# A recurrent layer and the network after it: from two stages to one

## The reference, cut to what matters

```python
q = x @ q_w.T; k = x @ k_w.T; v = x @ v_w.T          # 16 heads of 8
lc = sigmoid(tanh(x @ cs_w1.T + cs_b1) @ cs_w2.T + cs_b2)
lam = clip(sigmoid(decay_params) * (1 + 0.2 * lc), 0, 0.9995)
state = state * lam_t + k_t[:, None] * v_t[None, :]   # per head, 8 x 8, over 1024 tokens
y_t = q_t @ state;  s = y @ o_w.T
top1 = argmax(softmax(x @ gate_W.T + gate_b))         # one of 8 experts
inter = relu(x @ wi_W.T + wi_b + (x @ lora_A[top1].T) @ lora_B[top1].T)
g = silu(inter @ wo_W.T + wo_b)                       # 512 hidden
out = x_in + s * g
```

## Time and profile before

| | us |
|---|---|
| median of 3 runs (lowest, highest) | 1789.2 (1782.86, 1791.3) |
| the profiled execution's own time | 1788.66 |
| its span, first to last instruction | 1786.8 |
| layer 0 (`before_heads`, `attend`) | about 1520 |
| `recur`, from its first to its last instruction | about 191 |
| `finish` | about 76 |

### The profile page before, as it was taken

One profiled execution on the slowest core, in us unless ns is written; L12 is line 12 of the kernel. 1 busy time (PEld: TensorE's weight loads), 2 busy tenths in 40 slices (PEclk: granted clock), 3 DMA queues, 4 the chain that ended last, 5 costly groups with the idle time before them and its releaser, 6 DMA issues. The chain is left out here.

```text
span 1786.8 us, 38903 instructions
## 1 busy us (share of the span) xinstructions
PE 1631.6 (91%) x11942; PEld 909.4 (51%) x12100; DVE 1498.1 (84%) x3033; ACT 1149.5 (64%) x1755; POOL 1400.4 (78%) x804
## 2 busy tenths in 40 slices
PE   4879989858999999999999999999999998899888
PEld 3435654423555555555555555555555554466566
DVE  8778978986898988989889898898988988778831
ACT  6536534537887777887788777788778877312133
POOL 5576846847999999999999999999999997545421
PEclk9899999988999999999999999999999999889999
DMA  5466856769899889889889889889889888100001
GB/s 164 127 183 191 226 154 169 197 203 189 173 199 212 186 189 219 186 177 234 187 175 232 177 188 225 182 186 220 191 184 222 189 177 174 46 0 1 1 7 42
DMA packets 732914, 294.09 MB, mean 165 GB/s; under 512 B 629088, under 2 KB 696674, under 8 KB 732848
## 3 DMA queue, kind: packets, MB, share of 16 engines
q1 hardware_dynamic: 730048, 289.80, 72.1%
q0 software_dynamic: 2048, 3.15, 0.9%
q10 hardware_dynamic: 768, 0.53, 0.1%
HBM read 101.34 MB, written 58.85 MB: 90 GB/s over the span
## 5 line engine op out<-in xcount | busy, mean ns | idle before, releaser
L1270 POOL TENSOR_TENSOR probs_lo<-probs 128x1024 bf16<-128x1024 f32 x512 | 953.6, 1895 | 80.5 <-ACT probs L1234 80.0
L1234 ACT ACTIVATE probs<-scores,neg_max 128x1024 f32<-128x1024 f32 x512 | 588.3, 1149 | 220.1 <-DVE neg_max L1152 211.4
L1152 DVE CUSTOM_DVE_ANT_0 scores<-score_ps,bias_tab 128x1024 f32<-128x1024 f32 x512 | 620.5, 1220 | 76.9 <-issue 69.8
L1082 PEld LDWEIGHTS turn_ps<-ident_bf,probs 128*128 128x128 bf16 x4096 | 261.2, 98 | 146.1 <-issue 55.9
L1066 PE MATMUL score_ps<-x 128*128 128x512 bf16 x866 | 273.9, 384 | 48.9 <-PEq L293 18.2
L1082 PE MATMUL turn_ps<-ident_bf,probs 128*128 128x128 bf16 x4096 | 314.4, 220 | 0.2
L1101 PE MATMUL pv_ps<-probs_t_hi,v_hi_lo 128*128 128x512 bf16 x1024 | 263.8, 381 | 0.3 <-DVE share L1184 0.3
L1241 ACT COPY probs_t_hi<-turn_ps 128x1024 bf16<-128x1024 bf16 x256 | 253.8, 991 | 0.0
L438 POOL TENSOR_TENSOR qk_parts<-rotated,qk_parts 128x1024 bf16<-128x1024 f32 x64 | 137.4, 2151 | 87.7 <-ACT qk_parts L871 87.3
L1167 DVE COPY probs_t_hi<-turn_ps 128x1024 bf16<-128x1024 bf16 x256 | 172.7, 675 | 0.8 <-PE turn_ps L1082 0.8
L1074 PE MATMUL score_ps<-x 64*128 64x512 bf16 x1024 | 155.9, 383 | 0.0
(11 more groups left out here) (218 smaller groups left out, 2316.3 us busy)
## 6 DMA issues: line engine op xcount, KB each, us to landing
x<-qk_parts SPq DMA_DIRECT2D x192, 256.0 KB, 3.3
qk_parts<-qk_parts SPq DMA_DIRECT2D x252, 128.0 KB, 2.6
v_hi_lo<-v_parts SPq DMA_DIRECT2D x64, 256.0 KB, 3.1
bias_tab<-bias_by_distance SPq DMA_DIRECT2D x64, 240.0 KB, 3.8
v_parts<-bias_tab SPq DMA_DIRECT2D x52, 256.0 KB, 3.0
probs_t_lo<-probs_lo SPq DMA_TRANSPOSE x512, 3.2
g<-in_x SPq DMA_DIRECT2D x4, 512.0 KB, 6.3
dispatch<-dispatched SPq DMA_DIRECT2D x8, 256.0 KB, 3.4
```

The costliest lines, as they stand in the source:

```text
L1082: mm = pe.transpose(tp[n % 2][:, k, :], PRB[n % NP][:, k * P:k * P + P], ident16[:])
L1152: v.tensor_tensor_reduce(SB[n % 2][:], sp_[n % 2][:], TB[s][:, j:j + S], -SCALE, 3.0e38, ALU.add, ALU.min, neg_max[:, n % 16:n % 16 + 1]). ...
L1234: act.activation(PR[n % NP][:], SB[n % 2][:], ACT.Exp, bias=neg_max[:, m:m + 1], scale=-1.0, accum_out=row_sum[:, m:m + 1]).then_inc(exped, 1)
L1270: g.tensor_tensor(LQ[n % NL][:], PR[n % NP][:], PRB[n % NP], ALU.subtract).then_inc(low_made, 1)
```

## The change

`recur` and `finish` become one block, `layer1`. The jobs between the steps are handed out by a new function, `steps_of_layer1`, which also spreads the network's jobs, `zt` (transposes of masked z), `hid` (a hidden tile) and `out` (an output block), over steps 4 to 31 by a weight of 1, 2 and 7. They use the two `aux_ps` banks too, since the made rows and the share hold the other six. A bank is free when its taker has it: ACT for most jobs, DVE for `v`, `zt` and `out`.

- From batch 1 on the repeated value rows are not made by an fp32 matmul. A job `v` makes the 128 values once; ACT and DVE and POOL split them into three bf16 parts (high on ACT, remainder on DVE, middle on ACT, low on POOL), 24 DMAs a batch (`stack`) put the three parts of one column under one another in 48 rows of `v_stacked`, and two bf16 matmuls with a pattern of ones (`head_rows`, made on POOL) repeat and add them.
- `best_gate` and `route` work on one batch each: `best_gate` behind steps 1, 4, 12, 20, `route` two steps later. ACT's exp is between them.
- The norm is applied by ACT (scale and shift a tile), no longer by DVE; POOL makes the shift.
- silu, the product and the sum are done by batch; of batches 0 to 2 the product and sum are POOL's (`add_share`), of the last one DVE's.
- Table loads on ACT from the start of layer 1 on: 3 before, 11 now.

The diff, cut to its core:

```diff
+def steps_of_layer1():
+
+    at = [[] for _ in range(FE * B)]
+    at[0] += [("q", 0, 0), ("q", 0, 1)]
+    at[1] += [("z", 0, 0)]
+    for b in range(1, B):
+        n = FE * (b - 1)
+        for f, jobs in enumerate(([("turn", b, 0), ("turn", b, 1)], [("z", b, 0), ("c1", b, 0)], [("c1", b, 1), ("k", b, 0)],
+                                  [("k", b, 1), ("c2", b, 0)], [("c2", b, 1)], [("q", b, 0)], [("q", b, 1)])):
+            at[n + f] += jobs
+    for b in range(1, B):
+        for c in range(2):
+            at[FE * (b - 1) + 1 + c].append(("v", b, c))
+    feed = [("zt", 0, 0)] + [("hid", 0, i) for i in range(FT)]
+    for j in range(NR):
+        if j + 1 < NR:
+            feed.append(("zt", j + 1, 0))
+        feed.append(("out", j, 0))
+        if j + 1 < NR:
+            feed += [("hid", j + 1, i) for i in range(FT)]
+    cost = {"zt": 1, "hid": 2, "out": 7}
+    total, done, span = sum(cost[job[0]] for job in feed), 0, FE * B - FFN_FROM
+    for job in feed:
+        at[FFN_FROM + done * span // total].append(job)
+        done += cost[job[0]]
...
         @block.sync
...
+            def stack(b):
+                sp.wait_ge(v_lo, 2 * b)
+                if b >= 3:
+                    sp.wait_ge(made, FE * (b - 1))
+                for f in range(FE):
+                    for p in range(3):
+                        to = 64 * (f % 2) + H * p
+                        sp.dma_start(VP[b % 2][to:to + H, f // 2, :],
+                                     V3[H * f:H * f + H, p, :]).then_inc(vp_in[b % 2], DMA)
...
         @block.vector
...
+            for n in range(N):
+                scan(n)
+                for job in steps[n]:
+                    take(job)
+                if n % FE == 2 and n // FE + 2 < B:
+                    stats(n // FE + 2)
+                if n in GATE_AT:
+                    best_gate(GATE_AT.index(n))
+                if n - 2 in GATE_AT:
+                    route(GATE_AT.index(n - 2))
+                if n == 1:
+                    split_lora()
...
         @block.gpsimd
...
+                g.tensor_tensor(WT[:, n % 2, :], SC[:, n % 2, :], QT[:, b % 2, :], ALU.mult).then_inc(weighed, 1)
+                if n == 0:
+                    head_rows()
+                for kind, i, c in steps[n - 1] if n >= 1 else ():
+                    if kind == "v":
+                        v_low(i, c)
+                if f == 3 and b + 2 < B:
+                    rstd(b + 2)
+                if n == 4:
+                    join(3)
+                if n - 1 in SILU_AT[:B - 1]:
+                    add_share(SILU_AT.index(n - 1))
...
         @block.scalar
...
+            norm(0)
+            for job in first:
+                take(job)
...
+            norm(1)
+            act.wait_ge(fin_in, 7 * DMA)
+            for n in range(N):
+                for job in steps[n]:
+                    if job[0] != "out":
+                        take(job)
+                for kind, b, c in steps[n]:
+                    if kind == "v":
+                        middle(b, c)
+                if n % FE == 1 and n >= FE:
+                    take_share(n // FE - 1)
+                if n - 1 in GATE_AT:
...
+                    act.activation(lg, lg, ACT.Exp).then_inc(exp_ready, 1)
+                if n % FE == 5 and n // FE + 2 < B:
+                    norm(n // FE + 2)
+                if n in SILU_AT:
+                    gate(SILU_AT.index(n))
...
         @block.tensor
...
+                    if n < FE:
+                        mm = pe.matmul(pj[n % 2][:, half(c)], wv[:, f, :], tokens(b, c),
+                                       start=True, stop=True)
+                    else:
+                        mm = pe.matmul(pj[n % 2][:, half(c)], SEL[at, :, :].rearrange("r h e -> r (h e)"),
+                                       VP[b % 2][at, f // 2, half(c)], start=True, stop=True)
...
+                elif kind == "zt":
+                    pe.wait_ge(zm_ready, b // 2 + 1)
+                    for t in range(4):
+                        mm = pe.transpose(dst[0:3 * ER, t * P:t * P + P], ZM[:, 4 * (b % 4) + t, :], K.ident[:])
+                elif kind == "hid":
+                    pe.wait_ge(by_dve, dve_nth["zt", b, 0])
```

More of the change, by code:

```diff
@@ L42 @@
 DMA = 16
+FE, FFN_FROM = 8, 4
 MAGIC = 12582912.0
@@ L1322, in recur, with bank, half, rows @@
     ax = [ps(f"aux_ps{i}", [P, CH]) for i in range(2)]
-    FE = 8
     N = B * FE
[L1325 to L1341, removed]
+    first, steps = steps_of_layer1()
+    jobs = first + [job for step in steps for job in step]
+    place = {job: a for a, job in enumerate(jobs)}
+    step_of = {job: n for n, step in enumerate(steps) for job in step}
+    act_takes = [job for job in jobs if job[0] != "out"]
+    dve_takes = [job for job in jobs if job[0] in ("v", "zt", "out")]
+    act_nth = {job: k + 1 for k, job in enumerate(act_takes)}
+    dve_nth = {job: k + 1 for k, job in enumerate(dve_takes)}
+    GATE_AT = [1] + [FE * (b - 1) + 4 for b in range(1, B)]
+    SILU_AT = [step_of["out", 2 * b + 1, 0] + 1 for b in range(B)]
+    def bank(job):
+        return ax[place[job] % 2]
+    def half(c):
+        return slice(c * CH, c * CH + CH)
+    def rows(b):
+        return slice(b * BT, b * BT + BT)
+    def tokens(b, c):
+        return XNT[:, b * S + c * CH:b * S + c * CH + CH]
+    def vp_due(b):
+        return 3 * DMA * FE * len(range(2 - b % 2, b + 1, 2))
     with nc.Block() as block:
@@ L1386, in route @@
-            def route():
-                v.wait_ge(exp_ready, 1)
+                for t in range(b * BT, b * BT + BT):
+                    ins = v.bn_stats(st.six[:, t, :], X1[:, t, :])
+                ch.link(ins)
+                for t in range(b * BT, b * BT + BT):
+                    ins = v.bn_aggr(st.mean_var[:, t, :], st.six[:, t, :])
+                ch.link(ins)
+                ch.link(v.tensor_scalar(back[:, rows(b)], st.mean_var[:, rows(b), 0], -1.0, None, ALU.mult))
+                v.tensor_scalar(st.var[:, rows(b)], st.mean_var[:, rows(b), 1], 1e-5, None, ALU.add).then_inc(var_ready, 1)
@@ new lines, in take, with middle, gate @@
+                ins.then_inc(by_act, 1)
+            def middle(b, c):
+                act.wait_ge(by_dve, dve_nth["v", b, c])
+                act.copy(V3[:, 1, half(c)], VR[:, half(c)]).then_inc(v_mid, 1)
+            def take_share(b):
+                act.wait_ge(shared, FE * (b + 1))
+                act.wait_ge(joined, B + 1)
+                act.copy(S1[:, rows(b), :], so[:]).then_inc(s1_out, 1)
+            def gate(b):
+                act.wait_ge(by_dve, dve_nth["out", 2 * b + 1, 0])
+                act.activation(Y[:, rows(b), :], Y[:, rows(b), :], ACT.Silu).then_inc(gated, 1)
@@ L1532, in _ @@
+            if SILU_AT[B - 1] >= N:
+                gate(B - 1)
         @block.tensor
```

423 lines of the change are left out of this document (194 added, 229 removed).

## The result

The changed kernel takes 1766.2 us (median of 4 runs, 1762.2 to 1770.7), the kernel before 1789.7 in the same comparison: ratio **0.9885**, 95% interval 0.9862 to 0.9908, so faster by 1.2%. Forecast were 1761 us and a range of 1738 to 1783. The profiled execution took 1762.21 us, its span is 1760.5.

A forecast was written before the change was run, and what follows sets the result against it. PE was taken to set the pace of both stages. Ideal span 1733.9 us, plus 10.9 for the first z turn, 5 for clock and 9.3 for ACT's order, gave 1759.1; with 1.9 over span, 1761 us, range 1738 to 1783.

The forecast's parts named there:

- PE's work: From step 1 on, PE's priced jobs sum to 181.2 us, with bf16 made rows at 0.43 instead of 1.72.
- waits and half clock there: Added to PE's work: first z turn and hidden tile 10.9 us, low clock 5, ACT's order 9.3.
- rest: The end, behind step 31's made rows: hand-overs +2.8 us, then last products, sums and store 5.5.
- a turn: PE's transposes, read as 8 passes where a share has 16, priced at 0.45 us.
- The first z turn: In step 4, PE waits 7.0 us for route, then 3.8 at the hidden tile: together +10.9, +5 to +15.
- the stalled addition: Route's second operation on DVE, beside POOL's 2.35 us product, takes 2.49 us instead of some 0.4.
- Clock: PE's clock falls after the two close waits in step 4, counted as one: +5 us, between 0 and 12.
- ACT in order: ACT's added work and table loads free PE's banks late, in steps 10, 11 and 17 to 19: +9.3 us, 3 to 18.
- v by DMA: Stacking by 24 transfers a batch, 0.45 us each to issue, 11 us, costs nothing; later batches have some 20 us to spare.
- Rival 2: DVE becomes a partner in the bound; 11 takes of bank results at 1.5 us each give 1777. Chance 0.18.
- Rivals 3 and 4: PE idles at every bank DVE takes, 1798, chance 0.04; stacking transfers land one after another, 1817, chance 0.03.
- PE's 26 us of work: PE's passes over 24 steps: 31 us leave with the cheaper made rows, 5 come with the v jobs.

The follow-up runs named there:

- full rows: Changed kernel with the made rows of batches 1 to 3 contracted over all 128 rows, unused ones zero, instead of 48: 1755.7 us, ratio 0.9836.
- Parts alone: Changed kernel's bf16 parts, ACT norm and routing by batch, but the network in its own stage behind the recurrence as before: 1789.5 us, ratio 1.0018 to the kernel before.
- first jobs later: Changed kernel with 128-row made rows and padded lam network, plus the network's first jobs moved one or two steps later: 1764.5 us, ratio 0.9878.
- the padded network: Kernel with 128-row made rows, first z turn in step 5 and other network jobs from step 6, plus lam network zero-padded to 128 columns and rows: 1759.7 us.

## Why the prediction came out right

The forecast of 1761 lies 5 us under the median and 1.2 under the profiled run; the mechanism held, and two terms were off in opposite directions, so that the sum came out this near is in part luck. Forecast for the layer: 1759.1 - 1520.75 = 238.35. Measured: 245.17. The profiled span of 1760.5 agrees better than that only because the unchanged code ahead was 5.4 us shorter in this profile.

| stretch | forecast | measured | off |
|---|---|---|---|
| start to made rows of step 1 | 23.65 | 22.81 | -0.8 |
| PE's work, to made rows of step 31 | 175.4 | 187.7 | +12.3 |
| waits and half clock there | 25.2 | 18.5 | -6.7 |
| rest | 14.1 | 16.2 | +2.1 |

(The measured work is 206.19 less 15.5 of waits less some 3 of half clock at step 4; the forecast one is 181.2 less the last three shares and a pair of made rows.)

**PE's work, the mis-sized term.** The step was: "They contract 48 rows, the row's 96; I take its price." 0.43 became 0.53, and the pieces on both sides pay as well: 24 x 0.3 = 7 us, of which full rows gave back 6. The 12 us by kind of job, start to start and without the half clock of step 4: shares +2.7, made rows +2.4, k, q and v jobs +1.7, 12 c1 and c2 jobs +1.3 (1.02 where I had 0.92), z and turns +1.1, hidden tiles +2.6, outputs +0.3. The 7 are the first two and the jobs that stand behind made rows. The hidden tiles pay beside waits too: one that starts behind a wait took 0.96 instead of 0.86, and a low-rank part with a wait behind it 0.38 instead of 0.22. The reading of a turn was off as well: it has 4 passes (x4 in the timeline) and not 8; 0.45 was right for a z turn (0.44), but a pair of turns of normed tiles took 1.09. I had read the earlier trace rows, where a 96-row tile stands between tiles of 128, as the nearest row; the nearest was in the earlier trace rows, where two c1 jobs (32 columns) and the share behind them cost more than a q pair and its share. The Trainium skill (TensorEngine Tiling (Array Packing), "Key Properties") says that changing the tiling mode, and not just the tile, drains TensorE. The trace fits that, with a price of 0.1 us on each of the pieces around a change, but doesn't show a drain as such. Nothing of the kind shows at 96 rows: a hidden tile's low-rank part is 0.22 in both the earlier trace rows and the new stage.

**The first z turn** was forecast to wait 7.0 and the hidden tile 3.8; they waited 4.4 and 3.1. The routing ended 49.2 us into the layer instead of 52.0: it took 5.1 us from scan 3's end, forecast were 7.3. The 2.38 us of the stalled addition (L1466, forecast 2.49) were right, and the comparison behind it (L1468) was held up by POOL's v part, 0.82 instead of 0.22; pow, 1.65 us beside DVE, stopped nothing: the four small products (L1470) took 0.26 to 0.27 each beside it, as they do alone. The Trainium skill (SBUF — State Buffer, "SBUF: two separate sides") has the port pair of VectorE and GpSimd as a lock held for a whole instruction. The addition ends with POOL's product, 2.38 against 2.34, which agrees; the four products beside pow don't, and there the measurement decides.

**Clock**: +5 forecast; some 3 at step 4, and 1.6 at the last share, which was not forecast and stands in the row "rest".

**ACT in order**: 9.3 forecast; waits for lam, cs_hidden, k_t, xn_t and fhid 6.0, batch 3's turn 1.2, banks of v 0.8, so 8.0. Removing the switches gave 3.4 to 4.9. By place: steps 17 to 19, where the forecast had 4, gave 2.3, and steps 10 and 11, where it had 2.8, gave 1.8.

**v by DMA**: nothing, as forecast, but with luck. An issue took 0.63 us and not 0.45, so a batch's 24 took 15.8 us and not 11, and batch 2's began late. Its transfers, the median time to landing, and the made rows that need them:

```profile
1630.87 15.83 SPq L1413 DMA_DIRECT2D v_stacked<-v_three  x24
...
v_stacked<-v_three SPq DMA_DIRECT2D x72, 32.0 KB, 1.9
...
1650.02 0.60 PE L1713 MATMUL made_ps<-v_stacked,head_rows 48*128 48x512 bf16 x2
```

The last one, issued at 1646.11, landed at 1648.1, 1.9 us ahead of its use, where the forecast had "some 20 us to spare"; with full rows 0.9 us were left. A kernel that is faster still on PE may wait here. Parts alone did: the slack was the network's jobs.

**Rivals.** Rival 2 gave a price for DVE as a partner, 11 takes at 1.5. Most takes were hidden, but from scan 3 to the first take DVE is the bound (12.4 us busy of 12.7), which I had not said of any stretch. Rivals 3 and 4 did not come. The claim that the gain is PE's 26 us of work was too simple: alone, the cheap rows brought nothing.

**What stays open**: why the clock stays low longer at the start of some profiles (the start takes 15.4 to 15.8 us in eight, at a granted clock of 0.67 or 0.68, 16.2 and 16.3 in two at 0.62 and 0.64, and 17.3 to 17.5 in three at 0.61), when a wait of 1.5 to 2.6 us costs the clock, and what the first jobs cost if all stood one step later.

## What to carry to other kernels

Price a new instruction by its neighbours too: what it does to the pieces ahead of and behind it, and fill a short contraction with zeros if its neighbours use the whole array. Cheaper work on the bounding engine pays only if something else is ready to take its place and its new supply chain has cover; try each part alone before crediting it. When two profiles differ, look at the granted clock step by step before giving the difference to the edit. Before moving a job that waits, look which engine is full in that stretch and what the job meets at its new place.

## What the hardware showed that I had not expected

- A made-rows pair of 48 rows between tiles of 128 cost TensorE 0.1 us in the piece ahead, 0.1 in the small tile (0.53 against 0.43 for the same 1024 bf16 columns) and 0.1 in the piece behind.
- Idle times near 2 us had no single outcome: the clock halved behind 1.99 (changed kernel, last share, 3.64 us), 1.90 (the output of 5.47 us) and 1.50 (hidden tile of step 11, first jobs later), and stayed full behind 1.88 (full rows, last share, 2.05 us), 2.20 (that same output with the padded network, 3.84 us) and 2.57 (first hidden tile of `finish` before, 1.13 us). So the 3.5 us that the prediction took for one wait from the earlier trace rows is no bound.
- A 64-column operation of VectorE with two inputs in SBUF takes 0.23 us alone and 2.38, 2.39 or 2.10 beside a product of GpSimd; beside GpSimd's pow it wasn't slowed.
- A table load takes 1.28 us, and the operation behind it starts 0.01 later in 8 of 11 cases; the other three had to wait for their input. The loads still cost PE time, as they stand between jobs that free its two banks: with four fewer, steps 0 to 31 took 3.4 us less.
